# A wait of GpSimd for its own gathered rows, at the end of each chunk of five gather passes

## What is computed

```python
# L2: sum over edges, no weights (pass g2p)
agg = jax.ops.segment_sum(x[src], dst, num_segments=N)
...
# L3, first convolution, 64 columns (pass gcnp; the weights are put into the table and the result)
out = jax.ops.segment_sum(h[src] * norm[:, None], dst, n)
...
# L1 (8 heads, pass g1) and L3 (4 heads, passes g2 and g3): attention over the edges of each target
e = alpha_s[src] + alpha_d[dst]
e = jnp.where(e > 0, e, NEG_SLOPE * e)
emax = jax.ops.segment_max(e, dst, n)
w = jnp.exp(e - emax[dst])
wsum = jax.ops.segment_sum(w, dst, n)
att = w / wsum[dst]
out = jax.ops.segment_sum(att[:, :, None] * h[src], dst, n)
```

## Time and profile before

| | us |
|---|---|
| timed executions | 10194.92, 10167.76, 10173.58 |
| median of them | 10173.58 |
| the profiled execution's own time | 10204.18 |
| its span in the trace | 10202.4 |

### The profile page before, as it was taken

One profiled execution on the slowest core, in us unless ns is written; L12 is line 12 of the kernel. 1 busy time (PEld: TensorE's weight loads), 2 busy tenths in 40 slices (PEclk: granted clock), 3 DMA queues, 4 the chain that ended last, 5 costly groups with the idle time before them and its releaser, 6 DMA issues. The chain is left out here.

```text
span 10202.4 us, 102334 instructions
## 1 busy us (share of the span) xinstructions
PE 5438.7 (53%) x21038; PEld 4110.9 (40%) x21039; DVE 4005.7 (39%) x8761; ACT 3369.3 (33%) x8126; POOL 4572.9 (45%) x5200
## 2 busy tenths in 40 slices
PE   2249844555543444547933333555555455554296
PEld 1146543444432333445633333344443344443264
DVE  4623384555570000243320000345546454456443
ACT  0032203333333333424523333133332233332253
POOL 4021106555506666223336665466652466661332
PEclk8569957677766777758955555567677677777598
DMA  1243203333313333122121111233331233331223
GB/s 48 120 175 136 67 17 98 89 90 89 91 47 101 93 93 91 42 77 69 57 68 23 23 23 21 65 92 88 91 87 57 70 91 89 90 91 50 99 62 116
DMA packets 428577, 787.32 MB, mean 77 GB/s; under 512 B 131656, under 2 KB 284202, under 8 KB 420018
## 3 DMA queue, kind: packets, MB, share of 16 engines
q0 software_dynamic: 208304, 506.99, 18.1%
q1 hardware_dynamic: 211266, 193.04, 6.3%
q10 hardware_dynamic: 8640, 83.73, 2.0%
HBM read 602.11 MB, written 187.19 MB: 77 GB/s over the span
## 5 line engine op out<-in xcount | busy, mean ns | idle before, releaser
L682 POOL DMA_INDIRECT g_rows<-table,src_idx x2352 | 2226.1, 946 | 1404.3 <-issue 670.1
L953 PE MATMUL g_p_win<-g_rows,g_hot 128*128 128x264 f32 (+1 forms) x4704 | 1553.5, 490 | 42.3 <-issue 34.8
L953 PEld LDWEIGHTS g_p_win<-g_rows,g_hot 128*128 128x128 f32 x4704 | 1104.4, 246 | 311.7 <-issue 72.1
L844 ACT ACTIVATE g_hot<-iota,near 128x128 f32<-128x128 f32 x2352 | 721.0, 387 | 1132.3 <-DMA f_own<-table 556.6
L682 POOL DMA_INDIRECT g2p_rows<-rows,src_idx x784 | 741.0, 945 | 369.1 <-issue 228.4
L682 POOL DMA_INDIRECT gcnp_rows<-table,src_idx x784 | 739.6, 943 | 371.1 <-issue 228.9
L760 DVE TENSOR_TENSOR g_rows<-g_rows,g_p_w 128x1792 f32<-128x1792 f32 x336 | 679.0, 2021 | 44.6 <-issue 14.6
L966 PE MATMUL g_p_f<-ones 1*128 1x4 f32 (+1 forms) x336 | 83.8, 318 | 785.7 <-issue 330.2
L767 DVE TENSOR_TENSOR agg<-agg,g2p_p_out 128x256 f32 x112 | 42.2, 418 | 1090.8 <-PE g2p_p_out L915 625.9
L767 DVE TENSOR_TENSOR agg<-agg,gcnp_p_out 128x64 f32 x112 | 20.3, 221 | 1119.5 <-PE gcnp_p_out L915 808.0
L953 PE MATMUL g2p_p_win<-g2p_rows,g2p_hot 128*128 128x256 f32 x1568 | 419.0, 433 | 73.4 <-DMA g2p_rows<-rows,src_idx 73.4
(11 more groups left out here) (636 smaller groups left out, 11874.0 us busy)
## 6 DMA issues: line engine op xcount, KB each, us to landing
g_rows<-table,src_idx POOLq DMA_INDIRECT x2352
expert_rows<-e_zero ACTq DMA_DIRECT2D x28, 1332.5 KB
c_row<-back SPq DMA_DIRECT2D x35, 896.0 KB, 10.3
e_xin<-expert_rows SPq DMA_DIRECT2D x210, 130.0 KB
f_own<-table SPq DMA_DIRECT2D x21, 896.0 KB, 5.0
table<-t_row SPq DMA_DIRECT2D x14, 910.0 KB
expert_rows<-e_zero ACTq DMA_DIRECT2D x10, 1261.0 KB
back<-agg ACTq DMA_DIRECT2D x7, 1792.0 KB, 34.2
```

The lines of the kernel that those rows point to most:

```text
L682: gp.indirect_dma_start(rows[:, s, j, 0:width + H], None, table, bass.IndirectOffsetOnAxis(g.src_idx[:, at:at + 1], 0)).then_inc(got[s], 16)
L844: last = nc.scalar.activation(hot[:, j, :], g.iota[:, :], ACT.Square, scale=-1.0, bias=g.near[:, bass.ds(c * J + j, 1)])
L953: last = nc.tensor.matmul(p_win[:, 0:W], hot[:, j, :], rows[:, s, j, :], start=(j == 0), stop=(j == J - 1))
```

## The change

One line is added to GpSimd's code in `gather_pass`. After the 14 reads of a chunk GpSimd waits until `got[s]` has reached what these reads bring it to: 224 for each chunk that has gone into the buffer, this one included. All five passes have it, at the end of each of their 56 chunks.

```diff
                     for j in range(J):
                         at = c * J + j
                         gp.indirect_dma_start(rows[:, s, j, 0:width + H], None, table, bass.IndirectOffsetOnAxis(g.src_idx[:, at:at + 1], 0)).then_inc(got[s], 16)
+                    gp.wait_ge(got[s], 16 * J * (c // R + 1))
```

## The result

The change makes the kernel **1.1% faster** on the chip of the first measurement: 10067.19 us (median of 4 runs, 10054.90 to 10082.98) against 10176.12 us (median of 4 runs of the kernel before there, 10167.76 to 10194.92), ratio 0.9891 with a 95% interval of 0.987 to 0.9912. The prediction said 10167 us and "no difference". Later experiments ran on five further chips, called the second to the sixth here (whether the first chip is one of them is not known), and on two of these the same change costs 5.2% (ratios 1.0526 and 1.0523).

What follows compares the result with a forecast made beforehand. The prediction took issue of 14 reads plus 2.1 us of silence, 19.6 us a chunk, as the bound. Only the threes in g2p and gcnp changed anything, -7 us, giving 10167 us on the median; range 10095 to 10235.

Steps and rivals of the forecast that it cites:

- The bound: Gather passes: issue of 14 reads, 17.5 us, and 2.1 us of silence after it, 19.6 us a chunk.
- the debt: GpSimd: each chunk of reads leaves some 2.1 us of silence to pass before TensorE's signals are seen.
- 225 of 275: Chunk boundaries in the five passes that already end in a real wait for `used`: 35 + 34 + 156.
- Cost nothing: At boundaries that already wait, the landing is over before `used` comes, so the added wait costs 0.
- g1, g2, g3 keep their times: Sign to look for in the three passes with attention weights: times unchanged within some us.
- The new smallest gap: Between chunks, from last issue to landed data: 2.1 us in g2p, 1.9 us in the other passes.
- The starts: First four or five unbroken chunks of each pass: idle total unchanged, 12.3 us before and after in g2p; effect nothing.
- The threes: g2p and gcnp: repeating gaps 2.8, 0.3, 5.1 become 2.8, 2.1, 3.1; 0.2 us less in each of 33, -7 us.
- The ends: End of each pass: the last chunk's wait is over before TensorE finishes, so the barrier does not see it; nothing.
- The straight line of gaps: GpSimd's waits of 2.77, 5.12, 9.01, 11.11 us after one to five unbroken chunks: 2.09 us for every further chunk.
- Signals get through: Rival: pauses let TensorE meet `used` in time in g2p and gcnp, -75 us, 10098; chance 0.20.
- Paid everywhere: Rival: the landing wait is paid on top at all 280 chunk ends, +588 us, 10762; chance 0.03.

Runs made afterwards that it cites:

- half-row: Against the kernel before, each read in g2p and gcnp fetches 64 rows in place of 128, two sums incomplete: 10208.58 us in one run.
- seven-read: Against the kernel before, g2p and gcnp issue 7 of 14 reads a chunk: 8066.82 and 8068.44 us on two chips, 9105.41 us on the sixth.
- the first experiment: Against the kernel before, the landing wait only in g1, g2 and g3: 10240.63 us on the second chip, ratio 0.9903.
- the pause in the middle: Against the changed kernel, a second landing wait behind the 7th read of each chunk: 10107.81 us, ratio 0.9922 to the kernel before.

## Why the prediction was wrong, step by step

- **The bound** (issue of 14 reads and 2.1 us of silence) held in g2p and gcnp on the chips with the debt. The half-row and seven-read kernels put it better: 1.42 us for each read, of which 1.25 lie between the starts of two reads. As a statement about the kernel it was too wide: on two chips there is no debt.
- **The step that failed** is "As built it is no instruction of its own: it sits on the first read of the next chunk". It was read from the order of instructions, which does not print separate waits. As built it splits the two waits, and the restart is 0.5 us slower at each boundary that waits for `used`. From it follows the next: "225 of 275", "Cost nothing", was wrong in both directions. In the passes with heads, behind the starts, the ordinary gaps grow from 3.03 to 3.42 us (152 of them, 60 us), but 41 gaps of 9.0 us shrink to one, 40 x 5.9 = 238 us; the difference is the 178 us of the table. That a read with two waits "starts when the later of them is met" is what the prediction built this on; measured, it starts 0.26 us after the rise with one wait and 0.77 us with the two as built. In g2p and gcnp only the cost is left.
- **"g1, g2, g3 keep their times"** was wrong by 141 us of reads, 153 with their ends. I had taken the shortest waits for all, "since their means are 4.7 us". A mean of 4.7 with a longest of 10.2 in the earlier trace rows was two kinds of gap, 3.0 and 9.0, and the second kind, which gave it all back, was never looked at.
- **The new smallest gap** was right: 2.03 to 2.08 for 2.1 in g2p, 1.69 for 1.9 in gcnp.
- **The starts** were right: in gcnp 4 x 0.30 + 11.36 and the 2.76 of the next boundary were 15.3 us, and 1.80 + 1.68 + 1.68 + 1.71 + 1.69 + 6.84 are 15.4 now. In g2p eight boundaries took 20.5 us and take 21.1, and the four of g1, g2 and g3 29.9 and now 28.5 together. The place of the due gap was not right: it comes at the sixth boundary in gcnp and the seventh in g2p, and not at the fifth; why is not shown.
- **The threes** became pairs. The free boundary's 0.3 became 2.1 and the gap behind it fell, as forecast, but to 3.80 and not to 3.1, and no 2.8 follows. A pair holds 2.03 + 3.80 = 5.83 us for two boundaries, 2.9 for each, where a three held 8.2, 2.73 for each. The 0.2 more at each of some 50 boundaries is most of the 12 us by which the gaps grow in each of the two passes, and the slower restart at every second boundary is enough for it. So their reads take 30 us more where I had 7 less.
- **The ends** were put at nothing, since only the wait behind the last chunk was weighed. But TensorE is less far behind when the reads end, and the five ends are 35 us shorter, 22 of them in g2p and gcnp. That the pauses do it is argued and not shown: on the second chip the kernel without a wait in g2p and gcnp (the first experiment) has ends of 21.6 and 31.0 us there. These two passes lose 7 us in all where I had a gain of 7, and that this is only 14 us off is luck, since an error of 37 us in their reads and one of 22 in their ends stand against each other.
- **The rivals.** "Signals get through", at 10098, came nearer to the measured 10067, but for the wrong passes: g2p and gcnp, where it did not happen. "Paid everywhere", chance 0.03 and 10762 us, is near what happens on two of the chips, at 478 us and not 588, but for another reason: GpSimd has no silence there in which the landing could pass. The straight line of gaps made me sure of the debt; that it might be a property of the one chip in the profile I had not asked.

## What to carry to other kernels

When an engine's waits have a mean far over their shortest, split them by length first: the long kind has its own cause and its own price. A second wait on an instruction is not free, and which of two waits stands in front decides how fast the engine restarts; here that was worth some 0.8%. When an engine that runs ahead is paused, look at the end of the pass too, where the others work off what they are behind. And a gain of 1% that rests on delayed signals should be measured on several chips before it is kept, since this one is a loss of 5% on others.

## What the runs showed of the hardware

- On four of the six chips (the first among them, which may be one of the later ones) a signal from TensorE takes effect on VectorE, ScalarE and GpSimd late while GpSimd issues indirect reads, and shortly after it stops: 7.1 and 8.2 us late in the rows of g1, 15.9 us in those of g2p. On the two others the lag is 0.13 us in the same place. The lateness lies before the counter's rise: in g2p the rise of `used` is recorded at 3594.29, 15.7 us behind the matmul's end at 3578.56, and ScalarE starts 0.13 us after it. The signals of landings are not late in this way: where GpSimd waits for a landing alone, the wait ends 2.0 to 2.15 us after the last issue on both kinds (1.6 to 1.8 in gcnp).
- On the same four chips the traces hold a small part of the rises of `got` that the reads make: 2582 of 12544 in g2p before, 13 to 22% in the full passes of most kernels, and more where a chunk has more silence or fewer reads (69% in g2p with the pause in the middle, 35% with seven reads). On the two others it is 99% and more (12512 of 12544). Whether rises come in lumps there or their records are lost, and whether recording them has a part in TensorE's lateness, no run tells.
- On those four the kernel before runs g2p and gcnp at 1.42 us for each indirect read, and the half-row kernel does so too, on the one such chip that it ran on, though its issue is shorter (0.946 or 0.899 us, plus 0.30). What is not issue is silence, 2.4 us for 14 reads, and a pause in the middle of a chunk counts as well as one at its end.
- When `used` comes last, a wait instruction of its own in front of a read that carries the other wait costs 0.5 us at the restart (0.77 against 0.26 us from the rise). When `used` sits on the read and the landing on the instruction in front, it costs nothing (0.26 us).
- Why chips differ, and what holds the rises that TensorE makes back, stays open. That the debt goes with the chip is argued from the kernels of one chip being alike, and no chip was met twice to try it.
